# Scores of two heads at once on row strips of TensorE, keys stored without padding, and one values step for each group of heads

## The reference

```python
x = x + 0.5 * ffn(layernorm(x))      # sum over 8 experts of (silu(x@Wg[e]) * (x@Wu[e])) @ Wd[e], FFN = 512
x = x + attention(layernorm(x))
x = x + 0.5 * ffn(layernorm(x))      # the same weights again

def attention(x):                    # 16 heads of 8 dimensions, causal, 512 positions
    q, k, v = heads(x @ w_q.T), heads(x @ w_k.T), heads(x @ w_v.T)
    q, k = rotary(q) / sqrt(8), rotary(k)
    rel = rel_emb[clip(key - query, -32, 32) + 32]
    scores = q . k + q . rel         # masked to key <= query
    p = softmax(scores)
    return (p @ v + p . rel) merged over heads @ w_o.T
```

## Time and profile before

| | |
|---|---|
| median of 3 runs | 1336.65 us |
| profiled execution | 1328.16 us |
| its span | 1326.4 us |
| TensorE busy | 1307.4 us, 99% |
| VectorE busy | 1212.7 us, 91% |
| ScalarE busy | 1062.8 us, 80% |
| GpSimd busy | 1061.4 us, 80% |

### The profile page before, as it was taken

One profiled execution on the slowest core, in us unless ns is written; L12 is line 12 of the kernel. 1 busy time (PEld: TensorE's weight loads), 2 busy tenths in 40 slices (PEclk: granted clock), 3 DMA queues, 4 the chain that ended last, 5 costly groups with the idle time before them and its releaser, 6 DMA issues. The chain is left out here.

```text
span 1326.4 us, 28468 instructions
## 1 busy us (share of the span) xinstructions
PE 1307.4 (99%) x8334; PEld 1051.4 (79%) x8334; DVE 1212.7 (91%) x2611; ACT 1062.8 (80%) x2099; POOL 1061.4 (80%) x979
## 2 busy tenths in 40 slices
PE   8999999999999999999999999999999999999998
PEld 6888888787778787778888778887888778888787
DVE  6887999999999999999999999999999999998665
ACT  6866888878888888888888888887888888887565
POOL 7976888879878887797787878788778887878565
PEclk9999999999999999999999999999999999999999
DMA  6503899999999999999999999999999999997100
GB/s 190 163 1 118 160 217 228 201 224 229 215 222 215 199 197 194 243 196 202 200 209 208 216 206 200 197 227 205 198 206 198 206 219 206 204 188 138 23 5 8
DMA packets 718555, 241.39 MB, mean 182 GB/s; under 512 B 652480, under 2 KB 681920, under 8 KB 718400
## 3 DMA queue, kind: packets, MB, share of 16 engines
q1 hardware_dynamic: 562240, 180.84, 68.0%
q10 hardware_dynamic: 156160, 58.74, 22.4%
HBM read 77.33 MB, written 69.86 MB: 111 GB/s over the span
## 5 line engine op out<-in xcount | busy, mean ns | idle before, releaser
L1247 POOL TENSOR_TENSOR hid_lo<-hid,hid_hi 128x512 fp32r<-128x512 f32 x511 | 658.8, 1297 | 174.2 <-ACT hid_hi L948 92.7
L942 ACT ACTIVATE hid<-work 128x512 f32<-128x512 f32 x512 | 306.2, 600 | 100.9 <-PE work L798 72.0
L948 ACT CAST hid_hi<-hid 128x512 fp32r<-128x512 f32 x512 | 316.2, 625 | 88.2 <-PE acc L814 55.4
L1073 DVE SCALAR_TENSOR_TENSOR hid<-hid,work 128x512 f32<-128x512 f32 x512 | 343.9, 679 | 44.3 <-ACT hid L942 43.7
L1079 DVE TENSOR_TENSOR hid<-hid,work 128x512 f32<-128x512 f32 x512 | 346.3, 680 | 23.8 <-PE work L732 20.5
L1262 POOL TENSOR_TENSOR probs<-exps,probs 128x512 f16<-128x512 f32 (+1 forms) x288 | 304.1, 1061 | 62.0 <-ACT probs L1004 58.9
L1181 DVE TENSOR_REDUCE negmax<-work 128x1 f32<-128x384 f32 (+3 forms) x352 | 219.5, 632 | 0.5
L993 ACT ACTIVATE exps<-work,negmax_shifted 128x512 f32<-128x512 f32 (+2 forms) x320 | 187.6, 601 | 37.6 <-DVE negmax_shifted L1187 27.1
L821 PE MATMUL acc<-hid_lo,wd 128*128 128x512 f32 x512 | 207.2, 409 | 1.2 <-POOL hid_lo L1247 1.1
L730 PE MATMUL work<-xt,wu 128*128 128x512 f32 x512 | 205.1, 401 | 3.0 <-DVE rope L1163 1.3
L813 PE MATMUL acc<-hid_hi,wd 128*128 128x512 f32 x512 | 203.0, 396 | 1.5 <-ACT xn L959 0.7
(11 more groups left out here) (100 smaller groups left out, 1735.0 us busy)
## 6 DMA issues: line engine op xcount, KB each, us to landing
rel_win<-rel_window_scratch ACTq DMA_DIRECT2D x128, 320.0 KB, 3.8
prob_window_scratch<-probs SPq DMA_DIRECT2D x384, 80.0 KB, 3.2
q_scratch<-rope SPq DMA_DIRECT2D x16, 512.0 KB, 4.0
qq<-q_scratch ACTq DMA_DIRECT2D x32, 256.0 KB, 3.6
k_scratch<-rope SPq DMA_DIRECT2D x16, 512.0 KB, 4.8
rel_window_scratch<-g_s SPq DMA_DIRECT2D x32, 256.0 KB, 3.3
k_pad<-k_scratch SPq DMA_DIRECT2D x128, 64.0 KB, 3.5
prob_window_scratch<-probs SPq DMA_DIRECT2D x32, 256.0 KB, 4.0
```

What stands on the lines that cost most here:

```text
L942: act.activation(hid[:, arg % HB, :], work[bank_of["gate", arg]][:, :], ACT.Tanh, scale=0.5).then_inc(s_tanh, 1)
L948: act.copy(hid_hi[:, arg % HH, :], hid[:, arg % HB, :]).then_inc(s_hhi, 1)
L1073: dve.scalar_tensor_tensor(out=hid[:, arg % HB, :], in0=hid[:, arg % HB, :], scalar=1.0, in1=work[bank_of["gate", arg]][:, :], op0=ALU.add ...
L1247: pool.tensor_tensor(hid_lo[:, arg % HH, :], hid[:, arg % HB, :], hid_hi[:, arg % HH, :].bitcast(F32), ALU.subtract).then_inc(s_hlo, 1)
```

## The change

q and k are now laid out by heads: head a of a group has rows 32a to 32a+31 of `qq` and of `kk`, which takes the place of `k_pad` (weights, rotary tables, `rel_g` and `lanes` are permuted on the host to fit). q and k are stored once and not twice, the copies being made by the load. The scores of tiles 1 to 3 are products of 32 rows: one for each head (tile 1: `scores` for the first head of a task, `second` for the other), ordered so that two products on different rows and for different banks stand next to each other (`leads` names the first of a pair). A `second` waits until both first heads are done, since it writes a bank in which one of them wrote. Tile 0 stays a product of 128 rows by 4x128 columns, with keys spread by a new GpSimd step `k_apart` (128x512), one for each group. The `zero` steps of `k_pad` are gone. The values of a group are one step of 80 products. TB goes from 8 to 12, HB from 4 to 5, a task's bank may be taken again from the task AHEAD = 4 before, 2 until now, in the planner's rule, and `LATER` has other numbers.

```diff
-    HB = 4
+    HB = 5
-    TB = 8
+    TB = 12
+    AHEAD = 4
+    def leads(k):
+        return k - (k % GK - 1) % 2 if k % GK else k
-    STAGES = ((0, 1, 2), (3,))
+    STAGES = ((0, 1, 2, 3),)
-    LATER = {"acc": -978.2, "attention_sum": -208.7, ...
+    LATER = {"acc": -864.2, "attention_sum": -258.8, ...
...
-            step("PE", 0.02 + columns / 2286, due[k], "scores", k, ("load_q", quad // NT),
-                 ("load_k", quad // NT), done_with(back(k, 2)))
+            reach = (i + 1) * P
+            head = leads(k)
+            step("PE", 0.02 if head != k else 0.1 + (columns if i == 0 else reach) / 2286, due[head], "scores", k,
+                 ("load_q", quad // NT), ("k_apart" if i == 0 else "load_k", quad // NT), done_with(back(k, AHEAD)),
+                 ordered=[("second", k - 1)] if k % GK == 3 else [])
+            if i == 1:
+                step("PE", 0.02 if head != k else 0.1 + reach / 2286, due[head], "second", k, ("scores", k),
+                     ordered=[("scores", head + 1)] if head == k else [])
...
-        k_pad = sb("k_pad", [P, 2, HQ, L], F32R)
+        kk = sb("kk", [P, 2, L], F32R)
+        k_apart = sb("k_apart", [P, HQ, P], F32R)
...
-                    for a in range(HQ):
-                        sp.dma_start(k_pad[a:P:HQ, arg % 2, a, :].bitcast(F32),
-                                     bass.AP(k_t, t % VB * 4 * P * L + g * L + a * HG * L,
-                                             [[H * L, 4 * DH], [1, L]])).then_inc(s_kld[arg % 2], 16)
+                    for part in (HI, LO):
+                        sp.dma_start(kk[part:P:2, arg % 2, :].bitcast(F32),
+                                     bass.AP(k_t, (t % VB * 2 + part) * P * L + g * L,
+                                             [[HG * L, R], [0, 2], [1, L]])).then_inc(s_kld[arg % 2], 16)
...
-                    pe.matmul(bank[:, 0:len(places) * keys], qq[:, gg % 2, i * P:(i + 1) * P],
-                              k_pad[:, gg % 2, places[0]:places[-1] + 1, 0:keys],
-                              start=True, stop=True).then_inc(s_sc, 1)
+                        pe.wait_ge(s_ka, gg + 1)
+                        pe.matmul(bank[:, 0:HQ * P], q_tile, k_apart[:, :, :], start=True, stop=True).then_inc(s_sc, 1)
+                    else:
+                        if arg % GK == 1:
+                            pe.wait_ge(s_kld[gg % 2], 32 * (gg // 2 + 1))
+                        rows = slice(R * places[0], R * (places[0] + 1))
+                        pe.matmul(bank[:, 0:keys], q_tile[rows, :], kk[rows, gg % 2, 0:keys],
+                                  start=True, stop=True).then_inc(s_first if i == 1 else s_sc, 1)
+                if name == "second":
+                    bank = work[bank_of["scores", arg]]
+                    if leads(arg) == arg:
+                        pe.wait_ge(s_first, 2 * (gg + 1))
+                    rows = slice(R * places[1], R * (places[1] + 1))
+                    pe.matmul(bank[:, keys:2 * keys], q_tile[rows, :], kk[rows, gg % 2, 0:keys],
+                              start=True, stop=True, skip_group_check=True).then_inc(s_sc, 1)
...
+                if name == "k_apart":
+                    pool.wait_ge(s_kld[arg % 2], 32 * (arg // 2 + 1))
+                    if arg:
+                        pool.wait_ge(s_sc, GK * (arg - 1) + 1)
+                    pool.tensor_tensor(k_apart[:, :, :],
+                                       kk[:, arg % 2, None, 0:P].bitcast(F32).to_broadcast([P, HQ, P]),
+                                       lanes[:, 2:2 + HQ, None].to_broadcast([P, HQ, P]), ALU.mult).then_inc(s_ka, 1)
```

More of the change, by code:

```diff
@@ L104, in macaron_kernel @@
     LANDS = {"PE": 0.35, "ACT": 0.35, "DVE": 0.35, "POOL": 0.35, "SP": 2.6}
[L108 to L118, removed]
@@ new lines, in macaron_kernel @@
+    LATER = {"acc": -864.2, "attention_sum": -258.8, "band_turn": -293.2, "band_values": -778.7, "constants":
+             1425.0, "denominators": -158.1, "down": 42.0, "down_lo": 17.1, "exp": -391.8, "fill": 251.5, "gate": 30.1,
+             "gated": 139.2, "hi": 111.6, "k_apart": -774.6, "largest": -76.7, "ln_hi": -692.5, "ln_lo": -1018.7,
+             "ln_rstd": 1375.8, "ln_scaled": 331.6, "ln_stats": -1719.7, "ln_turned": -247.4, "lo": -786.3, "load_band":
+             -1126.3, "load_expert": -222.4, "load_k": -63.9, "load_q": -870.5, "load_window": 748.8, "load_x": -553.1,
+             "near": -217.3, "outproj": -128.9, "p_hi": -680.1, "p_lent": -925.5, "p_lo": -1659.9, "p_turn": 410.2,
+             "prepare_hi": 460.1, "prepare_lo": -477.7, "product": 163.6, "project": -207.4, "project_v": 60.9, "qk_hi":
+             -1264.6, "qk_lo": -941.2, "qk_store": -351.7, "qrel": -556.0, "qrel_copy": -338.0, "qrel_store": -734.6,
+             "recip": -1210.4, "rotate": 1217.5, "scale": -1302.7, "scores": 45.4, "second": -227.7, "shift": -813.3,
+             "split_hi": -347.1, "split_lo": 89.1, "spread": -540.5, "store": 168.8, "store_band": -439.6, "sum": 217.6,
+             "sum_turned": 48.1, "tanh": -536.1, "up": 32.4, "v_add": 0.1, "v_split": -247.8, "values": 28.0}
@@ L244, in macaron_kernel @@
                  ("scores", GK * (gg - 1) - 1 if gg >= 2 else None), lands=LATE + 1)
-            step("SP", 1.8, first - 14, "load_k", gg, ("qk_store", (t, 1)), ("zero", 7),
+            step("SP", 1.1, first - 14, "load_k", gg, ("qk_store", (t, 1)),
                  ("scores", GK * (gg - 1) - 1 if gg >= 2 else None), lands=LATE + 1)
+            step("POOL", 1.2, first - 6, "k_apart", gg, ("load_k", gg), ("scores", GK * (gg - 1) if gg else None))
             step("PE", 0.45, first - 22, "qrel", gg, ("load_q", gg))
@@ L351, in macaron_kernel @@
         if engine == "PE":
-            after_short = name == "scores" and TASKS[arg % NK][1] < 2
+            after_short = name in ("scores", "second")
         open_steps[engine].remove((time, key))
@@ L868, in _ @@
                     done.then_inc(s_g, 1)
-                if name == "scores":
+                if name in ("scores", "second"):
                     quad, i, places, keys = task(arg)
                     gg = quad // NT
+                    q_tile = qq[:, gg % 2, i * P:(i + 1) * P]
+                if name == "scores":
                     bank = take_bank(name, arg)
@@ L1321 @@
     window = np.repeat(np.where(w > i + R, 1e30, 0.0), HQ, axis=1)
-    lanes = np.repeat([[0.0, 1.0], [1.0, -1.0], [0.0, 1.0], [1.0, -1.0]], DH * HQ, axis=0)
+    lanes = np.tile([[0.0, 1.0], [1.0, -1.0], [0.0, 1.0], [1.0, -1.0]], (DH * HQ, 1))
+    lanes = np.concatenate([lanes, np.repeat(np.eye(HQ), R, axis=0)], axis=1)
     arrays = {
```

63 lines of the change are left out of this document (31 added, 32 removed).

## The result

The changed kernel takes 1374.3 us in the median of 4 runs (1372.01 to 1376.23), the kernel before beside it 1336.4. The ratio is 1.0288 with a 95% interval of 1.0239 to 1.0336: it is slower by some 38 us. The forecast was 1322.5 us, and the outcome is its first rival, the full price of the switch, which was put at 1384 us. The two profiled executions (1328.16 and 1372.01 us) lie 43.8 us apart, more than the medians: the kernel before spreads from 1329 to 1341 us, and its profiled execution lies at the low end.

A forecast was written before the change was run, and what follows sets the result against it. TensorE was taken as the bound, VectorE next. Columns -26.7, values -10.1 and switches +20.2 made -16.6 us; 3 given back left -14, profiled 1314, plus 8.5 gave 1322.5 us; own range 1315 to 1330, 8 in 10 1306 to 1388.

The forecast's parts named there:

- first rival: TensorE's 32-row runs: drains and uncovered weight loads, 0.43 us a run, 96 us against 36.8 saved; 1384 us, chance 0.25.
- h: TensorE: what one run of 32-row products costs beyond its columns, taken as 0.09 us, 20.2 us for 224 runs.
- the wait into values alone: TensorE: the 0.09 us lost going into the narrow values products, without the loads' part, used as the switch price.
- 26.7 + 10.1 saved: TensorE: 26.7 us less for score columns of tiles 1 to 3, 10.1 us less for merged values steps.
- Columns: TensorE, scores of tiles 1 to 3: paired products on different rows share their time, 65.4 us becomes 38.7, 26.7 less.
- Values: TensorE: one values step per group in place of two saves 32 x 0.316 = 10.1 us.
- GpSimd: k_apart adds 41.5 us of work at 1.3 us each, 4.1 us of memset goes; costed at nothing for the time.
- DMA: Halved k and q stores: gain bounded by 2 us of TensorE's waits for DMA, taken as 0.
- VectorE and the hidden waits: Attention section: with some 4% slack, VectorE gives back 3 us of TensorE's gain as waits, bounds 0 and 8.
- The stock of hidden waits: TensorE: some 48 us of short waits under modelled ends, span 1326 less modelled 1278, bands and start counted about 10.
- From span to median: Whole kernel: the runs' median stands 8.5 us above the profiled execution, carried over from before to reach 1322.5 us.

The follow-up runs named there:

- x_full_height: The changed kernel with plain copies for transposing DMAs, no causal mask, and the 32-row score products of tiles 1 to 3 made 128 rows high: 1316.4 us.
- x_full_height_two_values: x_full_height with the values of a group in two steps of 48 and 32 products, as before the change: 1329.6 us.
- the two replacements: Plain copies in place of the transposing DMAs and no causal mask, in the kernel before (1319.2 us) and in the changed kernel (1372.6 us).
- x_before: The kernel before with plain copies of the same bytes for all transposing DMAs and without the causal mask: 1319.2 us.

## Why the prediction was wrong

**The step that failed** is the one that chose h. "I take 0.09, the wait into values alone ... because row strips keep the 128 output columns and the form of the weights, and the loads of the pair go to rows that nothing uses twice." Measured h is 0.40 us a run in the kernel and by itself. The 224 runs cost 90 us and not 20, and 26.7 + 10.1 saved can't pay for it. The wait on the way in was sized rightly (0.09 to 0.10 us); what was left out was the same wait on the way out and the two uncovered f32 loads, some 0.10 each. The mechanism was priced in the same paragraph: drain (the wait until the running products are out), uncovered load in, drain, uncovered load out, 0.43. I had it from this kernel's own rows and set it aside by an argument on the shape for which no row stood. Going by the row nearest in kind, without cutting parts out of it, would have given the first rival: 1384 against 1374.3 measured. x_full_height shows the cause in the kernel itself: the same order without the strips takes 56 us less.

**The rule of the page**, that a change of tiling mode drains the engine ("TensorEngine Tiling (Array Packing)" of the Trainium skill, Key Properties), holds for row strips: no weight load starts for 0.35 us ahead of a run. The drains are about half, 0.21 of 0.40; the rest is the two f32 loads that the drains uncover.

**Columns.** Right: the two products of a pair share their time (one row of 0.50 us at 623.54), so the 26.7 us were real.

**Values.** The step of 80 costs 0.33 us beyond its products, 1.42 forecast and 1.43 measured in the sum (medians). The saving of 10 us has the rows of the steps behind it but no clean run; 13 us is what x_full_height_two_values shows, order included.

**GpSimd.** Right: `k_apart` takes 1.05 us (1.3 assumed), nobody waits for it, and shortening it changes nothing.

**DMA.** I took 0, bounded by 2 us of waits. What the halved stores give no run shows. But the two replacements gave the kernel before 14 us or more, so the 2 us of that view are too narrow a bound on what DMAs cost: some of it comes by way of other engines, and some lies under modelled ends.

**VectorE and the hidden waits.** The forecast had VectorE give back 3 us; it had to give nothing back, and went from 96 to 93%. The rival let 12 of 59 us be absorbed; the span rose by 43.8 us from 53 computed, some 5 of the tail added, so about 14 were. Without the transposes and the mask 53 of the same 58 us came through, so most of what was absorbed were waits that went with those two. The stock of hidden waits was itself put too high: 64 products of bands at 0.227 us and the first wait of 3.8 us are 18 us, not "about 10", which leaves some 40 us and not 48.

**From span to median.** The forecast added 8.5 us, the distance of median and profiled execution before. For the changed kernel that distance is 2.3 us (1374.3 against 1372.01). So the rival's +47 us stands against 43.8 between the profiled executions and 38 between the medians: its sum was better than its 1384 us looks.

**Not foreseen:** the idle time and the lower clock before the last pass, an estimated 4 to 5 us, in every kernel with the new order, and not in the kernel before. That the table LATER makes it was only argued, and the run for it could not tell.

**What the change brings without its strips:** x_full_height is 3 us under x_before (1316.4 against 1319.2), with the columns of before, one values step less for each group and the tail of the new order. Its scores being sums over heads, it is no version to use; and padded keys take the memory that twelve buffers need. No version that beats both kernels came out of the runs.

## What to carry to other kernels

Before small tiles are put between full ones, count the runs, not the products: here each run of 32 or 64 rows cost about 0.4 us with f32 weights and 0.21 with bf16, and a run of narrow bf16 outputs among f32 products 0.3. So a pair of 512 columns (0.23 us saved) can't pay. By these numbers a run of four strips of 512 columns would, by some 0.3 us (three products of 0.227 saved), and one of four strips of 256 would not (0.34 saved); that is an estimate for TensorE alone, and the one kernel that tried four strips lost more by its waits. A price measured in the same trace for a related switch is the forecast until a row says otherwise. And where a tuned table sets the order, an experiment that touches the planner's steps measures the table too; changing only operands keeps the order and the comparison clean.

## What the runs showed of the hardware

- A product on 96 or 100 rows among full ones costs nothing extra; one on 64 or 32 rows costs 0.38 to 0.41 us once for a run of any length tried (1 to 8 products, f32), and 0.21 us with bf16 weights.
- Strips of 32 rows on different rows start together, and their weight loads too: four took the time of one (1.326 against 1.320 us a repeat).
- 32 or 64 output columns at partition 0 in f32 cost nothing; 32 bf16 columns at partition 32 cost 0.29 us, 25 bf16 columns at partition 0 0.30. Which property decides isn't settled. f32 products followed by bf16 ones of full size lost nothing.
- Row strips directly followed by column strips cost 0.50 us, 0.2 less than apart.
- A product of 512 columns and 128 rows took 0.227 to 0.232 us with f32 weights and 0.216 with bf16.
- The order alone moved the same instructions from 1316.4 to 1703.2 us.
